# Graph attention into a spline layer on one core: a norm bound on t, low halves of h on GpSimd, one-column denominators, and weight halves a step apart

## What is computed

```
h = relu(layernorm(x))                       # 1250 x 512
HW = h @ W;  s = HW @ a[:512];  t = HW @ a[512:]
e = leaky_relu(s[row] + t[col], 0.2)         # one value for each edge
ex = exp(e - segment_max(e, row))
att = ex / segment_sum(ex, row)
agg = segment_sum(att * h[col], row)         # 1250 x 512
x = x + silu(agg) @ base_w.T + einsum(b_splines(agg), spline_w)   # 8 cubic splines per feature
```

## Time and profile before

| what | value |
|---|---|
| median of 3 runs | 684.4 us (683.07 to 684.95) |
| the profiled execution, its own time | 683.7 us |
| its span in the profile | 681.9 us |
| PE busy | 604.3 us, 89% of the span |
| DVE busy | 477.9 us, 70% |
| ACT busy | 371.5 us, 54% |
| POOL busy | 23.3 us, 3% |
| mean granted TensorE clock | 0.95 |

### The profile page before, as it was taken

How to read it: one execution, slowest core, us unless ns; L and a number is a source line. 1 busy time by engine, 2 the same in 40 slices (tenths; PEclk the granted TensorE clock), 3 DMA queues, 4 the chain that set the end, 5 groups by cost and what they waited for, 6 DMA issues and landing times.

```text
span 681.9 us, 8727 instructions
## 1 busy us (share of the span) xinstructions
PE 604.3 (89%) x3437; PEld 428.2 (63%) x3437; DVE 477.9 (70%) x739; ACT 371.5 (54%) x486; POOL 23.3 (3%) x30
## 2 busy tenths in 40 slices
PE   3766655999968999999999999869999999999994
PEld 2535643555534455555555555448999899988994
DVE  7989698999785999997369865784344434542354
ACT  1798597545779998987198620328331422332111
POOL 2000000000000000000000000202300020000000
PEclk9798686999979899999999999979999999999998
DMA  8553400000040000000001000090100000001202
GB/s 278 192 186 126 195 1 0 1 1 1 0 151 0 2 1 0 1 1 1 1 1 62 1 0 1 23 369 15 62 1 1 0 1 1 1 0 56 94 38 113
DMA packets 11417, 33.73 MB, mean 49 GB/s; under 512 B 718, under 2 KB 1038, under 8 KB 11120
## 3 DMA queue, kind: packets, MB, share of 16 engines
q1 hardware_dynamic: 11376, 33.17, 13.8%
HBM read 24.78 MB, written 8.40 MB: 49 GB/s over the span
## 4 chain that ended last, share of the span: by engine, by line
PE 67%; DVE 18%; ACT 8%; issue 4%; DVEq 1%; ACTq 1%; DMA 0%; SPq 0%
PE bank L1482 32%; PE bank L1557 20%; PE bank L1526 12%; DVE AL L994 2%; DVE OR L847 2%; DVE OM L850 2%; DVE EX L987 1%; DVE EX L999 1%; DVE SCR L958 1%; ACT CT L599 1%; PE bank L1328 1%; ACT JSQ L532 1%; ACT WKh L606 1%; DVE RDN L1029 1%; DVE hL L1004 1%
## 5 line engine op out<-in xcount | busy, mean ns | idle before, releaser
L1482 PE MATMUL bank<-BHL,WKh 128*128 128x418 f16 x1152 | 207.1, 342 | 4.2 <-DVE BHL L1083 4.2
L1482 PEld LDWEIGHTS bank<-BHL,WKh 128*128 128x128 f16 x1152 | 112.0, 97 | 99.3 <-DVE BHL L1083 4.6
L1557 PE MATMUL bank<-CF,YL 128*128 128x418 f32 x360 | 127.5, 354 | 0.0
L1557 PE MATMUL bank<-CF,YH 128*128 128x418 f32 x360 | 126.6, 352 | 0.0
L1277 DVE TENSOR_TENSOR Z<-bank,dvb 128x418 f32<-128x418 f32 x36 | 21.3, 593 | 69.1 <-PE bank L1557 69.1
L1557 PEld LDWEIGHTS bank<-CF,YL 128*128 128x128 f32 x360 | 67.6, 188 | 1.8
L1557 PEld LDWEIGHTS bank<-CF,YH 128*128 128x128 f32 x360 | 67.7, 188 | 1.0
L784 ACT ACTIVATE bnc<-bnm,tiny 128x1 f32<-128x1 f32 x12 | 3.5, 294 | 104.9 <-DVE bnm L1283 104.9
L1335 PE MATMUL bank<-OM,OR 128*128 128x160 f16 x320 | 32.3, 268 | 19.7 <-DVE OM L850 13.7
L1228 DVE SCALAR_TENSOR_TENSOR YL<-bank,dvc,YH 128x512 fp32r<-128x512 f32 x30 | 21.9, 748 | 38.5 <-ACT YH L765 38.5
L1526 PE MATMUL bank<-GWH,XH 128*128 128x512 f32 x120 | 48.1, 401 | 0.0
(11 more groups left out here) (202 smaller groups left out, 1010.6 us busy)
## 6 DMA issues: line engine op xcount, KB each, us to landing
WKf<-in_wk SPq DMA_DIRECT2D x9, 1024.0 KB, 5.4
c_scratch<-C SPq DMA_DIRECT2D x1, 3200.0 KB, 10.9
GWf<-in_gwT SPq DMA_DIRECT2D x3, 1024.0 KB, 5.4
C<-c_scratch SPq DMA_DIRECT2D x1, 2880.0 KB, 10.4
XT<-in_xT SPq DMA_DIRECT2D x1, 2500.0 KB, 8.8
x_scratch<-XT SPq DMA_DIRECT2D x1, 2500.0 KB, 16.1
XR<-x_scratch SPq DMA_DIRECT2D x1, 2500.0 KB, 8.9
outT<-Z SPq DMA_DIRECT2D x4, 625.0 KB, 3.1
```

The source lines that it names most:

```text
L1482: ins = mm(bank[:, 4 * (g % 2) + o, 0:G], lhs, rhs, start=(u == 0 and q == 0 and i == 0), stop=(u == UNITS - 1 and q == PAIR - 1 and i == 2))
L1557: ins = mm(bank[:, YB + u % YB, 0:G], Y[:, j, o * P:(o + 1) * P], CF[:, j, g * G:(g + 1) * G], start=(j == 0 and i == 0), stop=(j == NT - ...
```

## The change

Part by part, in the order of the program:

- **Bound on t.** ACT no longer copies `WAB`: it squares and sums the t half of `W a` from PSUM (one 512-column activation) and takes a scaled square root, a bound on |t| by the norm of `W a` and of h. The bound is added to the t column before it is spread (`mx[:, 3]`), so the reduce over |t|, `U` and its ACT instruction go, and `largest` reads the spread row from PSUM. `projections` read `W a` from PSUM and run for t and s one after the other with no wait between. The masks have six buffers, their product is f16.
- **Order of preparation.** On PE: transposes of tile 0, spread of t, degrees, the other transposes on two banks instead of four. The spread of the inverse degrees follows the first `pq` spread. On ACT `sum_squares` 3 and 4 come after the first transposed tile; 5 to 8 move into steps n = 1, 3, 5, 7 of the attention loop; `attention_rows(2)` moves into step 0. The Exp table is loaded ahead of `attention_rows(0)`.
- **Low halves of h** are made by GpSimd, ten instructions after `t_cols`.
- **Denominators.** k = 0 goes from `attend`. `weight_sums(g)`, after the second feature block of a group, makes 4 parts x 10 tiles x 2 halves = 80 products of one column with CT and AL as weights. DVE clamps and inverts 4 columns, `sums_spread(g)` spreads them by four f32 matmuls of 128 columns, `denominator_row` copies the row to RDN.
- **Weights.** `weights_high(0..9)` run on ACT in steps 16 to 25, `weights_low(0..7)` on DVE in steps 17 to 24, one step behind; 8 and 9 after the loop. LATE_TURN moves to (1, 2, 2, 3, 3, 4, 5, 6).
- **Start of the spline layer.** `ks` has two buffers from its first item, the two silu halves of a group run back to back, `nearest(0)` and `clipped(0)` come before `middle(1)`.

```diff
@@ constants @@
+LATE_SQUARES = (1, 3, 5, 7)
+MASKS = 6
+PARTS = (0, P, 2 * P, G - P)
+FIRST_HALF = 16
+LOOP_LOWS = 8
-LATE_TURN = (0, 1, 2, 3, 4, 5, 5, 6)
+LATE_TURN = (1, 2, 2, 3, 3, 4, 5, 6)
...
@@ gpsimd @@
+            pool.wait_ge(counts_final, 1)
+            pool.wait_ge(sub_copied, GROUPS)
+            def feature_rest(t):
+                pool.wait_ge(h_high, t + 1)
+                nc.gpsimd.tensor_tensor(hL[:, t, :], hx[:, t, :], hH[:, t, :], ALU.subtract).then_inc(h_low, 1)
+            pool.wait_ge(t_cols, 1)
+            for t in range(NT):
+                feature_rest(t)
...
@@ scalar @@
-                    nc.scalar.copy(WAB[:, :, :], bank[:, 6:8, :]).then_inc(wa_set, 1)
+                    nc.scalar.activation(JST[:, 0, :], bank[:, 7, :], ACT.Square, accum_out=tb[:, 0:1])
+                    act.drain()
+                    nc.scalar.activation(tb[:, 1:2], tb[:, 0:1], ACT.Sqrt, bias=tiny[:, 0:1], scale=BOUND * D
+                                         ).then_inc(t_bound, 1)
...
-            act.wait_ge(t_spread, 1)
-            act.wait_ge(t_scale, 1)
-            nc.scalar.activation(U[:, :], bank[:, 0:3, :].rearrange("p b c -> p (b c)")[:, 0:NP], ACT.Identity,
-                                 bias=tb[:, 1:2]).then_inc(t_used, 1)
...
+                if n == 0:
+                    attention_rows(2)
+                if n in LATE_SQUARES:
+                    sum_squares(5 + LATE_SQUARES.index(n), JSQ3)
+                if FIRST_HALF <= n < FIRST_HALF + LATE:
+                    weights_high(n - FIRST_HALF)
...
             silu_of(0, 0)
-            weights_high(0)
-            weights_high(1)
+            silu_of(0, 1)
             silu_high(0, 0)
...
             act.wait_ge(agg_unit, (DC + 1) * NG)
-            act.wait_ge(agg_out, DC)
             middle(0)
+            nearest(0)
+            clipped(0)
             middle(1)
-            nearest(0)
             nearest(1)
-            clipped(0)
-            weights_high(8)
-            weights_high(9)
...
@@ vector @@
             projections(1, 0, NT)
-            V.tensor_scalar(mx[:, 5, :], st[:, 1, :], LEAK, None, ALU.mult).then_inc(t_cols, 1)
+            dve.wait_ge(t_bound, 1)
+            V.tensor_scalar(mx[:, 3, :], st[:, 1, :], tb[:, 1:2], None, ALU.add).then_inc(t_cols, 1)
+            V.tensor_scalar(mx[:, 5, :], st[:, 1, :], LEAK, None, ALU.mult)
             dve.drain()
             V.tensor_tensor(mx[:, 4, :], st[:, 1, :], mx[:, 5, :], ALU.subtract)
-            projections(0, 0, 6)
-
+            dve.wait_ge(sub_counted, GROUPS)
+            projections(0, 0, NT)
+            V.tensor_scalar(mx[:, 1, :], st[:, 0, :], tb[:, 1:2], None, ALU.subtract)
             dve.wait_ge(t_spread, 1)
             trow = bank[:, 0:3, :].rearrange("p b c -> p (b c)")[:, 0:NP]
-            V.tensor_reduce(tb[:, 0:1], trow, AX, ALU.max, apply_absolute_value=True)
-            dve.drain()
-            V.tensor_scalar(tb[:, 1:2], tb[:, 0:1], 2.0, 1e-30, ALU.mult, ALU.add).then_inc(t_scale, 1)
-            projections(0, 6, NT)
...
             def denominators(g):
-                u = (DC + 1) * g
-                dve.wait_ge(agg_unit, u + 1)
+                dve.wait_ge(agg_unit, (DC + 1) * g + 3)
+                V.tensor_scalar(RDC[:, g, :], bank[:, att_bank(g, 0), DEN_AT:DEN_AT + len(PARTS)], 1e-30, None, ALU.max
+                                ).then_inc(den_out, 1)
+                dve.wait_ge(den_out, g + 1)
+                V.reciprocal(RDC[:, g, :], RDC[:, g, :]).then_inc(den_cols, 1)
...
+                if n == 13:
                     weight_scale()
-                if n == 12:
+                if n == 14:
                     denominators(0)
+                if n == 15:
+                    denominator_row(0)
                     aggregated(0, 0)
...
+                if FIRST_HALF < n <= FIRST_HALF + LOOP_LOWS:
+                    weights_low(n - FIRST_HALF - 1)
+                if n == 22:
+                    denominators(1)
...
@@ tensor @@
+            def weight_sums(g):
+                for i, c0 in enumerate(PARTS):
+                    out = bank[:, att_bank(g, 0), DEN_AT + i:DEN_AT + i + 1]
+                    for j in range(NT):
+                        for low in range(2):
+                            m = low_weights(g)[:, j, c0:c0 + P] if low else CT[:, j, g * G + c0:g * G + c0 + P]
+                            ins = mm(out, m, ones16[:, 0:1], start=(j == 0 and low == 0), stop=(j == NT - 1 and low == 1))
+                ins.then_inc(agg_unit, 1)
+            def sums_spread(g):
+                pe.wait_ge(den_cols, g + 1)
+                for i, c0 in enumerate(PARTS):
+                    ins = mm(bank[:, att_bank(g, 0), c0:c0 + P], down(RDC[:, g, i:i + 1]), ident[:, :], start=True, stop=True)
+                ins.then_inc(den_spread, 1)
...
+                    if k == 2:
+                        if g >= 1:
+                            pe.wait_ge(agg_out, DC * g)
+                        weight_sums(g)
+                    if k == 3:
+                        sums_spread(g)
...
-            pe.wait_ge(den_out, NG)
-            pe.wait_ge(agg_out, 2 * DC + 1)
+            pe.wait_ge(rden_set, NG)
+            pe.wait_ge(agg_out, 2 * DC)
```

More of the change, by code:

```diff
@@ L189, in build @@
         RDN = small("RDN", [G])
+        RDC = small("RDC", [NG, len(PARTS)])
         dvb_at = z5[0]
@@ L356, in fours, with low_weights, att_bank, pq_bank @@
             return onehot.rearrange("p k (a b) -> p k a b", b=FAN)
+        def low_weights(g):
+            return AL0 if g == 0 else AL12[:, g - 1, :, :]
+        def att_bank(g, k):
+            return (3, 4, 3)[g] if k == 0 else 4 * ((g + 1) % 2) + k - 1
+        def pq_bank(i):
+            return 0 if i == 2 else 6
         def twin(n):
@@ L370, in ks @@
         def ks(i):
-            return ks2[0 if i < NG + 1 else i % 2]
+            return ks2[i % 2]
         def silu_item(g, h):
@@ L554, in transposed @@
                     act.wait_ge(tposed, 2 * t + b + 1)
-                    nc.scalar.copy(CT[:, t, 5 * b * P:5 * (b + 1) * P], bank16[:, 4 + 2 * (t % 2) + b, 0:5 * P]
+                    nc.scalar.copy(CT[:, t, 5 * b * P:5 * (b + 1) * P], bank16[:, 4 + b, 0:5 * P]
                                    ).then_inc(tposed_out, 1)
-            for t in range(5):
-                transposed(t)
+            transposed(0)
+            sum_squares(3, JSQ)
+            sum_squares(4, JSQ)
             act.wait_ge(degs_done, 1)
             nc.scalar.activation(dvc[:, :], bank[:, 3, 0:NT], ACT.Sqrt, bias=1.0).then_inc(degs_out, 1)
-            act.wait_ge(t_spread, 1)
-            act.wait_ge(t_scale, 1)
-            nc.scalar.activation(U[:, :], bank[:, 0:3, :].rearrange("p b c -> p (b c)")[:, 0:NP], ACT.Identity,
-                                 bias=tb[:, 1:2]).then_inc(t_used, 1)
-            for t in range(5, NT):
+            act.wait_ge(squares, 5)
+            for t in range(1, NT):
                 transposed(t)
@@ L591, in exponentials, with weights_high @@
                                      ).then_inc(exps, 1)
+            def weights_high(u):
+                act.wait_ge(wscale_set, 1)
+                act.wait_ge(agg_unit, DC + 1)
+                if u >= 2:
+                    act.wait_ge(wk_low, u - 1)
+                nc.scalar.mul(weights(u)[:, 0, :], raw_weights(u), wsc[:, 0:1]).then_inc(wk_high, 1)
             exponentials(0)
@@ L924, in projections @@
                     dve.wait_ge(h_rows, t + 1)
-                    V.tensor_tensor_reduce(out=JH[:, t, :], in0=hx[:, t, :], in1=WAB[:, k, :], scale=1.0, scalar=0.0,
+                    V.tensor_tensor_reduce(out=JHs[k][:, t, :], in0=hx[:, t, :], in1=bank[:, 6 + k, :], scale=1.0, scalar=0.0,
                                            op0=ALU.mult, op1=ALU.add, accum_out=st[:, k, t:t + 1])
@@ L954, in largest @@
                     mask(s + 1)
[L955 to L956 removed]
+                if s >= 2:
+                    dve.wait_ge(masked, s - 1)
                 dve.wait_ge(mask_set, s + 1)
[L958 removed]
+                V.tensor_tensor_reduce(out=SCR[:, s % 2, :], in0=MSK[:, s % MASKS, :], in1=trow, scale=1.0, scalar=0.0,
                                        op0=ALU.mult, op1=ALU.max, accum_out=mx[:, 0, s:s + 1]).then_inc(masked, 1)
@@ L976, in _ @@
                 columns(i)
+                if i == 0:
+                    dve.wait_ge(degs_out, 1)
+                    V.reciprocal(dvc[:, :], dvc[:, :]).then_inc(dvc_set, 1)
             dve.wait_ge(c16_out, 16)
@@ L1383, in _, with degrees @@
             pe.wait_ge(consts_set, 2)
-            pe.wait_ge(wa_set, 1)
-            def degrees(t0, t1):
-                for t in range(t0, t1):
+            def degrees():
+                for t in range(NT):
                     for s in range(NT):
@@ L1460, in _ @@
                         attend(g, k, j)
+                    if g == 0 and k == 1:
+                        pe.wait_ge(sumsq_set, 1)
```

(4 more changed lines are left out.)

190 lines of the change are left out of this document (71 added, 119 removed).

## The result

The changed kernel takes 665.39 us as a median (664.74 to 666.76), the kernel before 684.12 in the same comparison: a ratio of 0.973, with a 95% interval from 0.9709 to 0.975. The profiled execution has a span of 665.0 us against 681.9.

The account below looks back on a forecast made before the run. PE alone sets the pace in the spline turns, so what moves the first turn counts. 3.2 (attention's end) + 8.6 (ACT free) + 3.1 (weights) + 2.8 (clock) = 17.7 us, giving 666.7 us; range 661 to 677.

Parts of the forecast that it names:

- First mask: DVE's masks ahead of attention begin at 79.9 us instead of 87.75, 7.85 us earlier; the spread of t is in time.
- GpSimd beside DVE: Ahead of attention, masks and small column operations on DVE wait for GpSimd's subtractions: 3.3 us lost, ends 0 and 7.
- First attention matmul: PE's start of attention comes at 107.8 us, 8.4 us earlier than 116.22.
- First group: Attention's first group: last low half near 128 us, PE waits 3.1 us for reciprocals, end at 140.2, 2.3 us ahead.
- the rival with 30%: Clock falls in the attention loop near one-column products: one costs 2.9 us, one per group 8.6, 669.6 to 675.3; 30%.
- One-column denominators: In each attention group 3.4 us of PE work replaces 3.5: PE gains nothing, DVE sheds a 2.77 us reciprocal.
- Groups two and three: In attention's later groups PE doesn't wait and ends at 189.4 us, 3.2 us earlier; DVE's cover is one microsecond.
- Into the turns: Between attention's end and the first turn: 8.6 us from ACT free at once, 3.1 from weights off the path.
- Clock at the first turn: PE waits 1.8 us before the first turn, less than 2.9, so the clock stays full: 2.86 us won.
- The pause feared for PE during the XT load: Beside the silu units PE's earlier 2.99 us pause might return under the XT load; 1.8 us of it covered.

Follow-up runs that it names:

- hl_early: The changed kernel with GpSimd's low halves of h started once their high halves are there, not after `t_cols`; median 664.26 us, ratio 0.9713.
- after_again: The changed kernel run and profiled again, unedited; median 666.13 us, ratio 0.9745.
- squares_spread: The changed kernel with two of four sums of squares moved from the attention loop into idle time of ScalarE; median 663.49 us, ratio 0.9712.
- wide_reciprocal: The changed kernel with an unused 418-column reciprocal put back on VectorE before the column reciprocals of groups 0 and 1; median 671.58 us, ratio 0.9818.
- hl_dve: The changed kernel with the low halves of h back on VectorE, in the first ten attention steps; median 664.5 us, ratio 0.972.
- den_first: The changed kernel with VectorE's column reciprocals, and the row copies and products that follow, one step earlier; median 664.22 us, ratio 0.9737.
- combined: The changed kernel with turn_high(0) and column reciprocals earlier, one sum of squares moved, low halves of h split between GpSimd and VectorE; median 658.56 us, ratio 0.9636.
- weights_after_b: The changed kernel with its first ten weight halves behind the attention loop, group 2's column reciprocals ahead of the fourth low half; median 673.42 us, ratio 0.9841.
- after: The changed kernel itself, in its first profiled execution (span 665.0 us); median 665.39 us, ratio 0.973.
- high_first: The changed kernel with ScalarE's rounding of the first spline turn moved ahead of clipped(2) and middle(3); median 665.11 us, ratio 0.9723.
- weights_after: The changed kernel with its first ten weight halves behind the attention loop again, group 2's column reciprocals behind eight low halves; median 676.24 us, ratio 0.9888.

## Why the prediction was right, point by point

The time was 665.4 for 666.7, and the sum of 17.7 us stands against 16.9 in the span. The mechanism was the predicted one: PE alone sets the pace from the first turn on, and the gain is what moved that turn, 15.7 us against 14.9. That the total came within 1.3 us is in part luck, since the errors of the terms offset each other. Its terms:

- **First mask** 79.9, measured 79.83: right. The spread of t was in time.
- **GpSimd beside DVE**, 3.3 us taken: the masks lost 2.05 and 0.67 us, the last column operation 0.24, together 3.0. The first small subtraction, charged with 1.1, escaped: it began at 73.06, GpSimd at 73.15. hl_early shows what it pays otherwise (1.03 us for 0.17). The others lost more than the 0.55 charged for each. The size was right by two errors against each other, which is luck. The Trainium skill, page "SBUF — State Buffer", section "SBUF: two separate sides", tells of a port pair that DVE and GpSimd share as an exclusive lock, held for a whole instruction. The traces agree: operations of ten columns stood for about the length of a GpSimd instruction (1.02 to 1.19 us beside 1.12), the masks for 0.7 to 1.0 us each, while projections (0.68) and the maximum (1.48), with their second input in PSUM, kept their times.
- **First attention matmul** 107.8, measured 106.36. The masks and maxima took less than before (one each 1.81 us for 1.93), which I had left unchanged; whether the second scratch row or the f16 product does this wasn't tried. The first exponential was at 103.6 and not at 105.0.
- **First group**: last low half at 126.7 for 128, PE's wait on the reciprocals 2.9 for 3.1. The places were right. Not taken into the sum was a fall of the clock in the loop, the rival with 30%: it came, once, in both profiled executions of the kernel. Behind the wait for RDC it costs about 1.6 us, not 2.9; ahead of it, in after_again, nothing. The reason given for it, one-column products beside the wait, isn't shown as the cause: in squares_spread the same products and the same wait left the clock at 1.00. Attention still ended 1.3 us before the predicted 189.4, since PE went on at 135.7 and not at 137.3, and the cheaper products below gave another 1.3.
- **One-column denominators**: 80 products in 1.98 us for 2.4, the eight passes in 0.89 for 1.0. PE thus gains 0.65 us a group, not nothing; by this alone 1.3 us in groups 1 and 2. wide_reciprocal shows the rest of the reading: DVE's time counts nearly in full.
- **Groups two and three**: PE didn't wait in the changed kernel, as predicted, and the cover was as thin as said: the column reciprocals of the second group were ready at 160.5 us, PE came to them at 161.5. The 2.76 us of wide_reciprocal made PE wait 1.35 us there.
- **Into the turns**: a gain of 11.7 us was predicted between the end of attention and the first turn, 11.1 measured. ACT began `middle(0)` 0.2 us after the end of attention instead of 8.7, 8.5 us for the predicted 8.6; from there to the turn it was 19.1 us instead of 21.7, 2.6 us for 3.1. The stop before the turn was 2.14 us for 1.8.
- **Clock at the first turn**, the term that was mis-sized: 2.86 us were to come back, 1.2 did. The step took the full clock for a stop shorter than the 2.9 us after which it had fallen before. It rested on one stop, and the earlier trace rows put that fall nearer to 2.6 us behind PE's last work (0.79 over 221 to 222). Here it fell in stops of 2.14 us, in five of nine executions, and full clock to the end would have been worth another 1.6 us.
- The pause feared for PE during the XT load didn't come: PE was busy for 15.00 of 15 us from 190 to 205 at a DMA share of 0.41.

What the parts are worth, by the experiments: the place of the weight halves 7 to 8 us against the order tried behind the loop, two wide reciprocals less in DVE's list 4.8 us and what the clock adds, GpSimd's low halves nothing or a loss. These don't add up to the 16.9 us and needn't, since each was tried in the changed kernel alone. The bound on t, the new order of preparation and the new start of the spline layer were not tried by themselves. For the first, hl_dve shows that an earlier start passes on: 3.0 us at the first exponential were 2.9 at the first turn, with the clock falling at the same places.

## What to carry to other kernels

Work given to an idle engine isn't free if it shares something with the one that it relieves: look at when it runs, not only at how long it takes, and beside which instructions of the other. Before costing a part on PE, ask which engine's list it stands in between two waits: here two reciprocals of 2.76 us put back into DVE's list cost PE 4.8 us, while the products that replaced them cost PE only 0.65 us a group less than the old ones, and the position of one instruction in an in-order list moved PE by 2 to 8 us. When a stretch is bound by two engines that hand work to each other, shortening one wait can show up partly as another, as in den_first; the four edits of combined, on three engines, together moved the first turn by 8.5 us of the 9.4 expected. And before reading a difference of 2 us from one profile, look where the clock fell: behind a wait a fall cost 1.6 us here, ahead of one it cost nothing.

## What the runs showed of the hardware

- A VectorE instruction on ten columns took 1.02 to 1.19 us instead of 0.16 to 0.23 beside GpSimd subtractions of 1.12 us, two masks together 2.88 us instead of 0.83. VectorE instructions with one input in PSUM weren't slowed (0.68 and 1.48 us, as alone). Ten GpSimd subtractions took 11.69 us when they ran beside masks, 11.18 when they didn't.
- Products of one column: 80 in 1.98 us at full clock, 0.025 each, and in 2.17 us at the 1.2 GHz level (group 0 of weights_after_b), so they hardly depend on the clock; the degrees before took 0.030 each at that level. 80 in a row at full clock left it at 1.00; 160 in a row, with PE never idle, brought it to 0.50 each of three times.
- A stop of PE of 2.13 or 2.14 us before the first turn was followed by the 1.2 GHz level in five of nine profiled executions, and in one of two of the same kernel; a fall cost 1.6 to 1.7 us. A wait of 2.9 us in group 0 was followed by it in four executions (after, hl_dve, high_first, weights_after) and not in squares_spread.
